# Adding a residual outside the matmul accumulation: x1 rebuilt by rows on GpSimd, added on VectorE

## The chip, the cores and the metric

The kernel runs on one core of a Trainium2 chip. The metric is the device time of one launch in microseconds (us). An execution under the profiler gives the rows that are read below.

## The reference

Sixteen sequences of 256 tokens and 128 channels, float32, go through one block with modulation from a small vector c. For each sequence:

```
h  = layernorm(x) * (1 + ca) + sa
a  = h + linear_attention(h) @ Wo + bo          # 16 heads of 8, elu+1 features
x1 = layernorm(a) * g1 + beta1                  # in the kernel: ny * g1 + beta1
z  = x1 + relu(x1 @ W1 + b1) @ W2 + b2
x  = x + ga * (layernorm(z) * g2 + beta2)
h2 = layernorm(x) * (1 + cb) + sb
x  = x + gb * sigmoid(mix_r(h2) @ Wr) * (square(relu(mix_k(h2) @ Wk)) @ Wv)
```

mix_r and mix_k blend each token with the one before it. The change concerns the x1 in the line of z.

## The kernel before

**Tiles.** A sequence is two chunks (c = 0, 1) of 128 tokens. Tensors "by rows" have tokens on the partitions (ny, z, x2: 128 x 2 x 128); transposed ones have channels on the partitions (hT, x1T: 128 x 256). The normalised rows without gain and shift are called ny. TensorE transposes them into a PSUM bank, and ScalarE turns that into x1T with the gain g1 per partition and the shift beta1 + b2 per partition (L300), so that b2 is already contained in x1T.

**The feed-forward part.** x1T is multiplied with W1 (`hidden_product`, L1018) into four blocks of hid. z is then accumulated in PSUM bank 6. `residual_into` (L980) transposes x1T back into rows as the first write of the accumulation, two 128x128 transposes per sequence; `feed_forward_out` (L986) adds 16 matmul instructions on top (eight products of float32, two instructions each). VectorE reads z out of bank 6 twice: `norm_stats` (L563) for mean and variance, and `centred` (L674), which forms z1 = (z - mean) * row. GpSimd makes rstd_z by a power (`norm_scale`, L453 and L457), and `middle` (L684) forms the new x from z1, rstd_z and xb.

**Stages.** The kernel is a software pipeline over t = 0 to 16, with the order of every engine's instructions written out by hand in a function `step(t)`. In step t, sequence t is at its first norm and attention, t-1 at the second half of attention and at y and ny, t-2 in the feed-forward part up to z, t-3 at z1, x2 and n3, and t-4 at the mixing part and the output. Sequence 15 goes through z in code of its own behind the loop, in chunks.

**Order around the change.** Engines synchronise by semaphores: a signal such as ny_ok is raised once per sequence, and `need(engine, signal, count)` waits for it. VectorE, in step t: stats of z of the previous step (`step_end`), den, rden, z1 (`centred`), att, k, x2 (`middle`), stats of n3, mixT, stats of ny, q, mv of ny, n3, kvs, and last ny (`normalise("ny")`, L578); then the next step starts with the stats of z. GpSimd, in step t: the scale of n1, the gate weights, the scale of n3, the scale of ny (sequence t-1), `plus_row` (L473), xb for t-2 (L484), the scale of z for t-2, and out_sb for t-4 (L491). TensorE starts step t with the transposes of n1, of ny (sequence t-2, written in step t-1) and of n3 (all L975), and ends it with z. In step 8 GpSimd also makes mix_now and mix_prev. ny, z1 and z's bank exist once each; the third of the hidden products of the next sequence goes into bank 6 as well and waits until z has been read (z1_ok).

**Queues.** Most loads are issued by SyncE. ScalarE issues c's columns, bk, bv and the mixing weights at the start.

Of the kernel before, what the change touches and what calls it, by code (L numbers as in the profile page):

```python
# [15 lines left out]
FF = 4  # L16
# [18 lines left out]
def build(nc, a, out, scratch):  # L35
    with ExitStack() as ctx:
# [3 lines left out]
        def sem(name):  # L40
# [62 lines left out]
        hid = sb("hid", [128, FF, L])  # L103
        z1 = sb("z1", [128, NC, D])
        xb = sb("xb", [128, NC, D])
        x2 = [sb(f"x2_{p}", [128, NC, D]) for p in range(2)]
# [51 lines left out]
         prod_ok) = map(sem, ("n1_ok ny_ok n3_ok k_ok q_ok wvm_ok kvs_ok den_ok rden_ok att_ok z1_ok x2_ok mix_ok "  # L158
                              "prod_ok").split())
        stats_ok = {n: sem(f"stats_ok_{n}") for n in NORMS}  # L160
        mv_ok = {n: sem(f"mv_ok_{n}") for n in NORMS}
# [95 lines left out]
        def _(act):  # L257
# [6 lines left out]
            act.wait_ge(pad_ok, 1)  # L264
            act.dma_start(bv_pad[0:1, :], a["bv"].rearrange("(a d) -> a d", a=1)).then_inc(bv_loaded, 16)
            act.dma_start(mix_w[:, :, :], a["mix_w"]).then_inc(mix_loaded, 16)

# [162 lines left out]
        def _(pool):  # L430
# [51 lines left out]
            def x_plus_shift(s, tile):  # L482
# [3 lines left out]
                                        ALU.add).then_inc(xb_ok, 1)  # L486

            def take_out(s):
                need(pool, stored[s % 2], 16 * (s // 2), 16 * S)
                need(pool, prod_ok, s + 1)  # L490
                nc.gpsimd.tensor_tensor(out_sb[s % 2][:, :, :], x2[s % 2][:, :, :], prod[:, :, :], ALU.add).then_inc(out_ok, 1)  # L491

            def step(t):
# [18 lines left out]
                if DIRECT <= t + 1 < S:  # L512
                    plus_row(t + 1)
                if live(t - 2):
                    need(pool, x2_ok, sd)
                    x_plus_shift(sd, xb)
                    if t < S:
                        norm_scale("z", sd + 1)
                    else:
                        tail_scale("z", slice(0, NC), 1)  # L520
# [28 lines left out]
        def _(dve):  # L549
# [25 lines left out]
            def normalise(name, dest, source, count, signal):  # L575
                need(dve, rstd_ok[name], count)
                for c in range(NC):
                    last = nc.vector.tensor_scalar(dest[:, c, :], source(c), mv[name][:, c, 0:1], rstd[name][:, c:c + 1],  # L578
                                                   ALU.subtract, ALU.mult)
                last.then_inc(signal, 1)  # L580
# [83 lines left out]
            def take_n3(t):  # L664
                sp_ = t - 3
                need(dve, h2T_mm, sp_)
                normalise("n3", n3, lambda c: x2[(t - 3) % 2][:, c, :], sp_ + 1, n3_ok)

            def centred(s):
                z = chunked(banks[6])  # L670
                need(dve, mv_ok["z"], s + 1)
                dve.wait_ge(gm_in[part_of(GM_PARTS, s)], 16)
                for c in range(NC):
                    last = nc.vector.scalar_tensor_tensor(z1[:, c, :], z[:, c, :], mv["z"][:, c, 0:1],  # L674
                                                          gm_rows[:, s, G_ROW, :], ALU.subtract, ALU.mult)
                last.then_inc(z1_ok, 1)
# [11 lines left out]
            def step_end(t):  # L688

                sd, sc = t - 2, t - 4  # L690
                z = chunked(banks[6])
                if live(t - 2):
                    need(dve, z_mm, sd + 1)
                    norm_stats("z", lambda c: z[:, c, :])
                if live(t - 4):
                    gated(sc)
                if live(t - 2):
                    norm_mv("z", sd + 1)
# [13 lines left out]
            def step(t):  # L712
                sa, sb_, sd, sp_, sc = t, t - 1, t - 2, t - 3, t - 4
                u = banks[1][:, 0:NC * (D + H)].rearrange("p (c e) -> p c e", c=NC)
                y = chunked(banks[1])
                z = chunked(banks[6])
                x2_p = x2[(t - 3) % 2]
# [156 lines left out]

            z = chunked(banks[6])
            dve.wait_ge(z_mm, LAST)
            norm_stats("z", lambda c: z[:, c, :])
            norm_mv("z", LAST)
# [31 lines left out]
        def _(pe):  # L910
# [72 lines left out]
            def feed_forward_out(f0, f1):  # L983
                for f in range(f0, f1):
                    for c in range(NC):
                        last = nc.tensor.matmul(banks[6][:, c * D:(c + 1) * D], hid[:, f, c * 128:(c + 1) * 128], w2[:, f, :],  # L986
                                                start=False, stop=(f == FF - 1 and c == NC - 1))
                return last
# [24 lines left out]
            def step(t):  # L1013
# [53 lines left out]
                if live(t - 2):  # L1067
# [5 lines left out]
                    if draining(t):  # L1073
                        need(pe, kvs_ok, S)
                        need(pe, hidb_ok, sd)
                    else:
                        need(pe, z1_ok, sd)
                    hidden_product(2)
# [27 lines left out]
                if live(t - 2):  # L1106
                    if draining(t):
                        need(pe, z1_ok, sd)
                        need(pe, hida_ok, sd + 1)
                    else:  # L1110
                        need(pe, hidb_ok, sd + 1)
                    for c in range(NC):
                        residual_into(banks[6], x1T, c)
                if live(t):
# [35 lines left out]
            for f in range(FF):  # L1150
# [3 lines left out]
                if f % 2 == 1:  # L1154
                    last.then_inc((w1a_mm, w1b_mm)[f // 2], 1)
            pe.wait_ge(z1_ok, LAST)
            for c in range(NC):
# [114 lines left out]
```

## Time and profile before

| | us |
|---|---|
| median of 3 runs | 168.03 (167.76 to 170.08) |
| the profiled execution | 168.26 |
| its span in the profile | 166.3 |
| TensorE busy | 157.8 (95%) |
| VectorE busy | 130.5 (78%) |
| ScalarE busy | 119.3 (72%) |
| GpSimd busy | 101.1 (61%) |

The time of an execution is 1.96 us above its span. "Busy" of TensorE counts overlapping matmuls up to the modelled end of each, so the distance between the starts of two groups says what one costs. The granted clock of TensorE is at full speed (1.00, its 2.4 GHz level) in the stretches of the loop. Names in the rows leave out buffer numbers: n1 and n3 both read "n", z1 reads "z", x2 reads "x", wv_gate and the others as they are.

### The profile page before, as it was taken

How to read it: one execution, taken by the hardware profiler on the slowest of the kernel's cores; microseconds unless marked ns; L12 is line 12 of the kernel's file. 1: busy time of each engine (PE TensorE's matmuls, PEld its weight loads, DVE VectorE, ACT ScalarE, POOL GpSimd, SP SyncE). 2: the span in 40 equal slices, each digit the busy share in tenths (PEclk: the TensorE clock that was granted, in tenths of full speed). 3: DMA queues.
4: the chain of work that ended last, by engine and by line, in shares of the span. 5: the costliest groups of instructions: out<-in, count | busy, mean ns of one | idle time of the engine just before them, and what ended most of it. 6: DMA issues, size and time to landing. Idle time of an engine off the chain costs nothing. (4 is left out here: it accounts for less than half of the span.)

```text
span 166.3 us, 4064 instructions
## 1 busy us (share of the span) xinstructions
PE 157.8 (95%) x1155; PEld 145.6 (88%) x1155; DVE 130.5 (78%) x589; ACT 119.3 (72%) x325; POOL 101.1 (61%) x236
## 2 busy tenths in 40 slices
PE   7989799999999999999999999999999999989882
PEld 7867689889999999999999999999999999878571
DVE  3565757789797979798889979897979797977852
ACT  4365685969696969698886969696969694846552
POOL 4333336676576767768597757675767645783531
PEclk9999999999999999999999999999999999999999
DMA  3838929900010101010010101010101010101012
GB/s 114 224 125 267 312 74 307 403 13 0 0 34 4 32 0 34 2 32 3 0 35 0 34 6 32 0 32 4 34 2 35 0 32 0 35 0 35 0 32 63
DMA packets 8173, 9.93 MB, mean 60 GB/s; under 512 B 692, under 2 KB 6360, under 8 KB 8152
## 3 DMA queue, kind: packets, MB, share of 16 engines
q1 hardware_dynamic: 7712, 9.41, 17.9%
q10 hardware_dynamic: 440, 0.28, 0.6%
q8 instruction: 9, 0.15, 0.4%
q14 instruction: 12, 0.10, 0.2%
HBM read 7.55 MB, written 2.13 MB: 58 GB/s over the span
## 5 line engine op out<-in xcount | busy, mean ns | idle before, releaser
L986 PE MATMUL bank<-w,hid 128*128 128x128 f32 x240 | 31.3, 275 | 0.0
L1018 PE MATMUL bank<-x1T,w 128*128 128x256 f32 x120 | 30.9, 380 | 0.0
L986 PEld LDWEIGHTS bank<-w,hid 128*128 128x128 f32 x240 | 29.2, 192 | 0.0
L296 ACT ACTIVATE hT<-bank,modT 128x256 f32<-128x256 f32 x16 | 9.0, 565 | 21.5 <-PE bank L975 21.4
L1018 PEld LDWEIGHTS bank<-x1T,w 128*128 128x128 f32 x120 | 21.5, 190 | 2.5 <-ACT x1T L300 0.2
L457 POOL TENSOR_TENSOR rstd_n<-vare_n,power 128x2 f32<-128x2 f32 x30 | 21.0, 702 | 2.3
L453 POOL TENSOR_TENSOR vare_n<-mv_n,eps 128x2 f32<-128x2 f32 x30 | 6.1, 204 | 20.2 <-DVE mv_n L572 20.2
L274 ACT ACTIVATE n<-x_all,shift_n,rstd_n 128x128 f32<-128x128 f32 x32 | 13.9, 486 | 2.7 <-POOL shift_n L465 2.5
L578 DVE TENSOR_SCALAR ny<-bank,mv_ny,rstd_ny 128x128 f32<-128x128 f32 x32 | 11.7, 406 | 4.6 <-POOL rstd_ny L457 4.2
L288 ACT ACTIVATE keepT<-bank,modT 128x255 f32<-128x255 f32 x28 | 14.3, 562 | 0.6 <-PE bank L975 0.6
L563 DVE BATCH_NORM_STATS2 stats_z<-bank 128x6 f32<-128x128 f32 x30 | 7.4, 289 | 8.5 <-PE bank L986 8.5
L453 POOL TENSOR_TENSOR vare_z<-mv_z,eps 128x2 f32<-128x2 f32 x14 | 2.7, 195 | 18.4 <-DVE mv_z L572 18.4
L975 PE MATMUL bank<-ident,n 128*128 128x128 f32 x62 | 12.1, 276 | 1.4 <-DVE n L578 0.8
L332 ACT ACTIVATE hid<-bank,b_cols 128x256 f32<-128x256 f32 x30 | 12.7, 484 | 0.0
L491 POOL TENSOR_TENSOR out_sb<-x,prod 128x256 f32<-128x256 f32 x15 | 10.9, 728 | 2.1 <-DVE prod L704 2.0
L709 DVE SCALAR_TENSOR_TENSOR mixT<-bank,modT,keepT 128x256 f32<-128x256 f32 x28 | 12.1, 471 | 0.0
L457 POOL TENSOR_TENSOR rstd_ny<-vare_ny,power 128x2 f32<-128x2 f32 x16 | 11.2, 699 | 1.3
L1099 PE MATMUL bank<-kqvo,attT 128*128 128x128 f32 x64 | 11.5, 275 | 0.0
L484 POOL TENSOR_TENSOR xb<-x_all,gm_rows 128x256 f32<-128x256 f32 x15 | 10.9, 724 | 0.2 <-DMA gm_rows<-mod_rows_dram 0.2
L684 DVE SCALAR_TENSOR_TENSOR x<-z,rstd_z,xb 128x128 f32<-128x128 f32 x30 | 10.0, 375 | 0.9 <-POOL out_sb L491 0.7
L300 ACT ACTIVATE x1T<-bank,beta_b,cols 128x256 f32<-128x256 f32 x15 | 8.4, 559 | 3.2 <-PE bank L975 3.2
L563 DVE BATCH_NORM_STATS2 stats_ny<-bank 128x6 f32<-128x128 f32 x32 | 7.8, 287 | 3.6 <-PE bank L1099 2.7
(185 smaller groups left out, 466.7 us busy)
## 6 DMA issues: line engine op xcount, KB each, us to landing
gm_rows<-mod_rows_dram SPq DMA_DIRECT2D x2, 960.0 KB, 8.9
out<-out_sb SPq DMA_DIRECT2D x15, 128.0 KB, 1.8
gm_rows<-mod_rows_dram SPq DMA_DIRECT2D x1, 768.0 KB, 6.1
w<-in_w SPq DMA_DIRECT2D x1, 512.0 KB, 6.7
bv_row<-bv_rows_dram SPq DMA_DIRECT2D x1, 512.0 KB, 10.0
x_all<-in_x SPq DMA_DIRECT2D x1, 384.0 KB, 5.7
bv_row<-bv_rows_dram SPq DMA_DIRECT2D x1, 384.0 KB, 3.5
gm_rows<-mod_rows_dram SPq DMA_DIRECT2D x1, 384.0 KB, 4.3
```

The source lines that it names most:

```text
L274: last = nc.scalar.activation(n1[s % 2][:, c, :], x_all[:, NC * s + c, :], ACT.Identity, scale=rstd["n1"][:, c:c + 1], bias=shift_n1[:, c: ...
L288: nc.scalar.activation(keepT[:, i, 1:L], banks[2][:, 0:L - 1], ACT.Identity, scale=mod_col(KEEP + i, s), bias=mod_col(SB, s)).then_inc((ke ...
L332: last = nc.scalar.activation(hid[:, f, :], hidden_bank(t)[:, (f - 2) * L:(f - 1) * L], ACT.Relu, bias=b1_cols[:, f:f + 1])
L457: nc.gpsimd.tensor_tensor(rstd[name][:, :], vare[name][:, :], power[:, :], ALU.pow).then_inc(rstd_ok[name], 1)
L484: nc.gpsimd.tensor_tensor(tile[:, :, :], x_all[:, NC * s:NC * (s + 1), :], gm_rows[:, s, GB_ROW:GB_ROW + 1, :].broadcast_to([128, NC, D]), ...
L563: ins = nc.vector.bn_stats(stats[name][:, c, :], source(c))
L578: last = nc.vector.tensor_scalar(dest[:, c, :], source(c), mv[name][:, c, 0:1], rstd[name][:, c:c + 1], ALU.subtract, ALU.mult)
L709: nc.vector.scalar_tensor_tensor(mixT[:, i, :], banks[2][:, 0:L], modT[:, MOVE + i, s:s + 1], keepT[:, i, :], ALU.mult, ALU.add).then_inc( ...
L975: last = nc.tensor.transpose(bank[:, c * 128:(c + 1) * 128], tile[:, c, :], ident[:, :])
L986: last = nc.tensor.matmul(banks[6][:, c * D:(c + 1) * D], hid[:, f, c * 128:(c + 1) * 128], w2[:, f, :], start=False, stop=(f == FF - 1 an ...
L1018: return nc.tensor.matmul(bank[:, f % 2 * L:(f % 2 + 1) * L], w1[:, f * 128:(f + 1) * 128], x1T[:, :], start=True, stop=True)
L1099: last = nc.tensor.matmul(banks[1][:, c * D:(c + 1) * D], attT[:, c * 128:(c + 1) * 128], wo, start=False, stop=(c == NC - 1))
```

## The change

x1 is also made by rows. The vectors g1, beta1 and b2 are loaded spread over all partitions. GpSimd multiplies ny by g1 and adds beta1 + b2; VectorE adds the result to z as it copies z from PSUM into a tile z_sb, and both later readers of z take z_sb. TensorE no longer transposes x1T back for sequences 0 to 14; sequence 15 keeps the old way. x1T itself stays, since W1 needs it.

```diff
+        z_sb = sb("z_sb", [128, NC, D])
+        x1_scaled, x1_rows = sb("x1_scaled", [128, NC, D]), sb("x1_rows", [128, NC, D])
+        g1_row, beta1_row, b2_row, shift_row = (sb(n, [128, D]) for n in ("g1_row", "beta1_row", "b2_row", "shift_row"))
...
 # ScalarE's queue, at the start
             act.dma_start(bv_pad[0:1, :], a["bv"].rearrange("(a d) -> a d", a=1)).then_inc(bv_loaded, 16)
+            for row, name in ((g1_row, "g1"), (beta1_row, "beta1"), (b2_row, "b2")):
+                act.dma_start(row[:, :], a[name].rearrange("(a d) -> a d", a=1).broadcast_to([128, D])).then_inc(rows_in, 16)
             act.dma_start(mix_w[:, :, :], a["mix_w"]).then_inc(mix_loaded, 16)
...
 # GpSimd
+            def x1_by_rows(s):
+                if s == 0:
+                    pool.wait_ge(rows_in, 48)
+                    nc.gpsimd.tensor_tensor(shift_row[:, :], beta1_row[:, :], b2_row[:, :], ALU.add).then_inc(shift_row_ok, 1)
+                pool.wait_ge(ny_ok, s + 1)
+                nc.gpsimd.tensor_tensor(x1_scaled[:, :, :], ny[:, :, :], g1_row[:, :].unsqueeze(1).broadcast_to([128, NC, D]),
+                                        ALU.mult).then_inc(x1s_ok, 1)
+                pool.wait_ge(x1s_ok, s + 1)
+                need(pool, zs_ok, s)
+                if s == 0:
+                    pool.wait_ge(shift_row_ok, 1)
+                nc.gpsimd.tensor_tensor(x1_rows[:, :, :], x1_scaled[:, :, :], shift_row[:, :].unsqueeze(1).broadcast_to([128, NC, D]),
+                                        ALU.add).then_inc(x1r_ok, 1)
...
                 if DIRECT <= t + 1 < S:
                     plus_row(t + 1)
                 if live(t - 2):
+                    x1_by_rows(sd)
                     need(pool, x2_ok, sd)
                     x_plus_shift(sd, xb)
...
 # VectorE
             def normalise(name, dest, source, count, signal):
                 need(dve, rstd_ok[name], count)
+                if name == "ny":
+                    need(dve, x1s_ok, count - 1)
...
+            def take_z(s):
+                dve.wait_ge(z_mm, s + 1)
+                dve.wait_ge(x1r_ok, s + 1)
+                nc.vector.tensor_tensor(z_sb[:, :, :], chunked(banks[6]), x1_rows[:, :, :], ALU.add).then_inc(zs_ok, 1)
+                dve.wait_ge(zs_ok, s + 1)
+                norm_stats("z", lambda c: z_sb[:, c, :])
+
             def centred(s):
-                z = chunked(banks[6])
+                z = z_sb
...
 # step_end, VectorE
                 if live(t - 2):
-                    need(dve, z_mm, sd + 1)
-                    norm_stats("z", lambda c: z[:, c, :])
+                    take_z(sd)
...
 # TensorE
-                                                start=False, stop=(f == FF - 1 and c == NC - 1))
+                                                start=(f == 0 and c == 0), stop=(f == FF - 1 and c == NC - 1))
...
                     else:
-                        need(pe, z1_ok, sd)
+                        need(pe, zs_ok, sd)
                     hidden_product(2)
...
-                    for c in range(NC):
-                        residual_into(banks[6], x1T, c)
```

The same replacement of z1_ok by zs_ok is made in the draining step and ahead of sequence 15's own z, and VectorE's code behind the loop calls take_z for sequence 14.

## Rows read from the trace of the kernel before

**Rows 1.** The page, busy time of each engine: us, share of the span, instructions.
```profile
PE 157.8 (95%) x1155; PEld 145.6 (88%) x1155; DVE 130.5 (78%) x589; ACT 119.3 (72%) x325; POOL 101.1 (61%) x236
```

**Rows 2.** Timeline of TensorE: start us, us, engine, line, operation, out<-in, count.
```profile
53.23 0.38 PE L975 MATMUL bank<-ident,ny 128*128 128x128 f32 x2
...
61.99 0.38 PE L975 MATMUL bank<-ident,ny 128*128 128x128 f32 x2
```

**Rows 3.** Timeline of TensorE: the residual's transposes and the group behind them.
```profile
59.08 0.38 PE L980 MATMUL bank<-ident,x1T 128*128 128x128 f32 x2
59.30 0.41 PE L1120 MATMUL bank<-wv_plus,a_sb 128*128 128x144 f32 x2
```

**Rows 4.** Timeline of VectorE, one period.
```profile
53.21 0.49 DVE L563 BATCH_NORM_STATS2 stats_z<-bank 128x6 f32<-128x128 f32 x2 [0.79 <-PE bank L986]
...
55.08 0.51 DVE L674 SCALAR_TENSOR_TENSOR z<-bank,mv_z,gm_rows 128x128 f32<-128x128 f32 x2
...
55.91 0.42 DVE L767 SCALAR_TENSOR_TENSOR k_sb<-exp_k,bank 128x256 f32<-128x256 f32 x1
56.24 0.61 DVE L684 SCALAR_TENSOR_TENSOR x<-z,rstd_z,xb 128x128 f32<-128x128 f32 x2
...
58.07 0.24 DVE L572 BATCH_NORM_AGGREGATE mv_n<-stats_n 128x2 f32<-128x6 f32 x2
58.40 0.49 DVE L563 BATCH_NORM_STATS2 stats_ny<-bank 128x6 f32<-128x128 f32 x2
...
59.14 0.24 DVE L572 BATCH_NORM_AGGREGATE mv_ny<-stats_ny 128x2 f32<-128x6 f32 x2
...
60.46 0.73 DVE L578 TENSOR_SCALAR ny<-bank,mv_ny,rstd_ny 128x128 f32<-128x128 f32 x2 [0.19 <-POOL rstd_ny L457]
61.98 0.49 DVE L563 BATCH_NORM_STATS2 stats_z<-bank 128x6 f32<-128x128 f32 x2 [0.79 <-PE bank L986]
```

**Rows 5.** Timeline of GpSimd in the same period and the next.
```profile
55.20 0.73 POOL L491 TENSOR_TENSOR out_sb<-x,prod 128x256 f32<-128x256 f32 x1
...
59.46 0.20 POOL L453 TENSOR_TENSOR vare_ny<-mv_ny,eps 128x2 f32<-128x2 f32 x1
59.73 0.69 POOL L457 TENSOR_TENSOR rstd_ny<-vare_ny,power 128x2 f32<-128x2 f32 x1
...
60.80 0.73 POOL L484 TENSOR_TENSOR xb<-x_all,gm_rows 128x256 f32<-128x256 f32 x1
63.03 0.19 POOL L453 TENSOR_TENSOR vare_z<-mv_z,eps 128x2 f32<-128x2 f32 x1 [1.50 <-DVE mv_z L572]
```

**Rows 6.** Timeline of VectorE, then of GpSimd, in the step with mix_prev.
```profile
82.55 1.20 DVE L684 SCALAR_TENSOR_TENSOR x<-z,rstd_z,xb 128x128 f32<-128x128 f32 x2
...
82.89 0.72 POOL L528 TENSOR_TENSOR mix_prev<-mix_w,mix_now 128x256 f32<-128x256 f32 x1
```

**Rows 7.** Timeline of ScalarE at the start.
```profile
5.85 0.88 ACT L274 ACTIVATE n<-x_all,shift_n,rstd_n 128x128 f32<-128x128 f32 x2 [2.51 <-POOL shift_n L465]
```

**Rows 8.** Timeline of VectorE, steps 2 to 4 and the last period's end.
```profile
25.66 0.25 DVE L572 BATCH_NORM_AGGREGATE mv_ny<-stats_ny 128x2 f32<-128x6 f32 x2
...
27.63 0.48 DVE L563 BATCH_NORM_STATS2 stats_z<-bank 128x6 f32<-128x128 f32 x2
...
32.78 0.49 DVE L563 BATCH_NORM_STATS2 stats_ny<-bank 128x6 f32<-128x128 f32 x2 [0.77 <-PE bank L1099]
...
35.49 0.48 DVE L563 BATCH_NORM_STATS2 stats_z<-bank 128x6 f32<-128x128 f32 x2
...
44.44 0.50 DVE L563 BATCH_NORM_STATS2 stats_z<-bank 128x6 f32<-128x128 f32 x2 [0.76 <-PE bank L986]
...
141.29 0.50 DVE L563 BATCH_NORM_STATS2 stats_z<-bank 128x6 f32<-128x128 f32 x2 [0.79 <-PE bank L986]
```

**Rows 9.** Timeline of VectorE, then of GpSimd, in the last step.
```profile
147.76 0.73 DVE L578 TENSOR_SCALAR ny<-bank,mv_ny,rstd_ny 128x128 f32<-128x128 f32 x2 [0.89 <-POOL rstd_ny L457]
...
148.61 0.72 POOL L484 TENSOR_TENSOR xb<-x_all,gm_rows 128x256 f32<-128x256 f32 x1
```

More of the change, by code:

```diff
@@ L159, in build @@
                               "prod_ok").split())
+        rows_in, shift_row_ok, x1s_ok, x1r_ok, zs_ok = map(sem, "rows_in shift_row_ok x1s_ok x1r_ok zs_ok".split())
         stats_ok = {n: sem(f"stats_ok_{n}") for n in NORMS}
@@ L690, in step_end @@
                 sd, sc = t - 2, t - 4
-                z = chunked(banks[6])
                 if live(t - 2):
-                    need(dve, z_mm, sd + 1)
-                    norm_stats("z", lambda c: z[:, c, :])
+                    take_z(sd)
                 if live(t - 4):
@@ L715, in step @@
                 y = chunked(banks[1])
-                z = chunked(banks[6])
                 x2_p = x2[(t - 3) % 2]
@@ L873, in out_of_last @@
                                         ALU.add).then_inc(out_last_ok[c], 1)
-            z = chunked(banks[6])
-            dve.wait_ge(z_mm, LAST)
-            norm_stats("z", lambda c: z[:, c, :])
+            take_z(LAST - 1)
             norm_mv("z", LAST)
@@ L1107, in step @@
                     if draining(t):
-                        need(pe, z1_ok, sd)
+                        need(pe, zs_ok, sd)
                         need(pe, hida_ok, sd + 1)
@@ L1155, in _ @@
                     last.then_inc((w1a_mm, w1b_mm)[f // 2], 1)
-            pe.wait_ge(z1_ok, LAST)
+            pe.wait_ge(zs_ok, LAST)
             for c in range(NC):
@@ L1259 @@
         "bv": attn["bv"],
+        "g1": attn["g1"],
+        "beta1": attn["beta1"],
+        "b2": attn["b2"],
     }
```

## The prediction

> **What bounds the kernel now.** I first read the busy totals: TensorE 95%, VectorE 78%, GpSimd 61% [rows 1]. That suggests that work taken off TensorE is gained and that GpSimd has room for more; whether it is so depends on where the work is put, so I went to the timeline of one step, engine by engine. On TensorE the transposes of ny start at 53.23 and 61.99: a period of 8.76 to 8.77 us with no idle time noted between them [rows 2]. VectorE shows the same 8.77 us from stats_z to stats_z (53.21 to 61.98), and in it a wait of 0.79 us for TensorE's z [rows 4]. From 44.44 to 141.29 [rows 8] there are eleven such periods, ten of 8.77 and one of 9.15 (the step in which GpSimd also makes mix_now and mix_prev). So TensorE sets the pace, but its lead is small: ny ends at 61.19 (60.46 + 0.73) and TensorE reads it at 61.99, a margin of 0.80 us [rows 2, 4].
>
> **TensorE's saving.** A pair of residual transposes moves the next group's start from 59.08 to 59.30 [rows 3]: 0.22 us per step, 15 steps, 3.3 us in all, if TensorE stays the bound. One matmul's duration there is no price, since they overlap (the pair lasts 0.38 us). The Trainium skill (TensorE: Matmul & The Clock Gate, Part 4: PE-mode transpose) gives about 275 ns for one transpose in a kernel; two of them per step would make the saving 8.3 us by that figure, and the start-to-start row decides against it.
>
> **The new wait of ny.** This is the step that decides. There is one buffer ny, and normalise("ny") of sequence t-1 now waits until GpSimd has read the ny of t-2 (x1s_ok). GpSimd does that reading in the same step t, behind the scale of ny (t-1) and plus_row. So ny (t-1) can't be written when its rstd is ready, but only after plus_row and a whole 128x256 pass.
> I count from the end of mv_ny, 59.14 + 0.24 = 59.38. Before: vare_ny at +0.08, ny at +1.08 [rows 4, 5]. New: x1_scaled starts where xb starts now, 60.80, +1.42; xb is the same form with a broadcast row, 0.73 us [rows 5], so it ends at +2.15; ny starts at +2.19 (a wait across engines costs 0.04, as rstd_ny to ny). That is 1.11 later, against a margin of 0.80, and ny ends at +2.92.
> x1_rows is one more 0.73: it waits for x1_scaled on its own engine (about 0.08, the spacing between vare and its rstd) and runs from +2.23 to +2.95. xb, and then vare_z, are queued behind both; vare_z was preceded by 1.50 us of idle time [rows 5], 1.46 of which x1_rows and x1_scaled take, and it waits for a later mv_z now anyway: nothing.
>
> **VectorE's add.** take_z needs x1_rows: it starts at +2.99. Nearest row: k_sb, 128x256 with one operand in PSUM, 0.42 us [rows 4]. Then a wait on its own result, 0.04: stats_z starts at +3.45. Before it was 61.98 - 59.38 = +2.60, of which 0.79 was the wait for TensorE. The cover of the add is thus gone.
> From stats_z to the end of mv_ny VectorE is in order and nearly gapless: 59.38 - 53.21 = 6.17, less 0.17 of waiting for y (stats_ny starts 0.33 after mv_n, where 0.16 is the usual spacing), 6.00 [rows 4]. The new loop is 6.00 + 3.45 = 9.45 us, against 8.55 for TensorE. bn_stats I take as equal from either memory, but z1 read from z_sb should look like x (0.61 a pair with SBUF operands) and not like z1 now (0.51) [rows 4]: +0.10, so 9.55.
>
> **z1 against GpSimd's out_sb.** z1 now takes z and the row both from SBUF. Where x, with the same operands, met mix_prev on GpSimd, its pair took 1.20 us instead of 0.61 and ended at 83.75, 0.14 after mix_prev [rows 6, 4]. In the ordinary step x meets only 128x2 instructions of GpSimd, and its 0.61 is undisturbed. z1 starts at 1.87 after stats_z and out_sb at 1.99 (55.08 and 55.20) [rows 4, 5], both hung on the same stats_z, so they will meet in every step. The first half of z1 is under way, the second waits until out_sb's 0.73 is over and ends at about +2.86 instead of +2.38: 0.48 in place of the 0.10, a period of 9.93. Bounds: 0 (GpSimd yields) to 0.75 (both halves wait). I take 0.48, the measured pattern.
> The Trainium skill (SBUF — State Buffer, Who interferes with whom) says that a VectorE instruction with two SBUF inputs and a GpSimd instruction that reads SBUF exclude each other; the trace agrees for x (1.20 against 0.61), and no row shows it for z1.
>
> **Start.** Three more loads are issued on ScalarE's queue, 64 KB written each. ScalarE's n1 waits 2.51 us for GpSimd there [rows 7]; three issues of up to 0.8 us each would fit. Their traffic beside x and the weights: 0 to 0.7 us, taken as 0. They are needed at 27 us, long landed. The first shift_row (128x128, 0.42) lies once in front of x1_scaled. In step 2 mv_ny ends at 25.91 and stats_z starts at 27.63, +1.72; new +3.45 + 0.42: 2.15 later. Step 3 is bound by latency (VectorE waits 0.77 for y) and gets the 1.1 of ny again; step 4, 35.49 to 44.44 = 8.95, becomes 9.5 [rows 8]. Together 3.7 us (rounded).
>
> **Middle.** Eleven periods at 9.93 = 109.2; less 0.42 in the last, which has no plus_row; plus 0.6 in the step with mix_prev, whose x is delayed as before but with no slack to take it: 109.4 against 96.85, +12.5.
>
> **End.** In the last step GpSimd scales n3 between ny and x1_scaled: x1_scaled takes xb's place at 148.61, ends at 149.34, and ny starts at 149.38 instead of 147.76 [rows 9]: +1.6. ny, n3, x and the last norms follow one another on VectorE from there, so the add counts too: +0.5. Total +2.1.
>
> **Sum.** 3.7 + 12.5 + 2.1 = 18.3 on the profiled execution's 168.26: 186.6. The median of the runs is 168.03, 0.23 lower: 186.3 us, 11% slower. TensorE's 3.3 us and the earlier release of z's bank (after the add instead of after z1) are worth nothing, as TensorE then waits 9.93 - 8.55 = 1.4 us per step for ny.
>
> **Rivals.**
> 1. The loop, without the meeting of z1 and out_sb (period 9.55): 11 x 0.38 = 4.2 less, 182.1. For it: which of the two waits depends on 0.12 us. Chance 0.27.
> 2. VectorE's order gives way and only the path through TensorE counts: ny's transposes to y's stats 5.17 (53.23 to 58.40), from there to the mean 0.98, then +2.95: 9.10 per period. 3.6 in the middle, 2.6 at the start, 2.1 at the end: about 176.5. Against it: VectorE's 6.00 has no gaps that I can see. Chance 0.09.
> 3. Not slower: GpSimd gets to x1_scaled early, so that the wait on x1s_ok is over before rstd_ny. TensorE stays the bound and saves up to 3.3 us: 164.7 to 168. It decides whether x1_scaled ends before 60.42 in a step like this one; GpSimd does have idle time (1.50 us), but after xb and not before, and its order is written out. Chance 0.08, half of it for a saving of 2% or a little more.
> 4. Worse than 190: GpSimd's two passes also hold up n3 or q on VectorE, or the first loads are late. Chance 0.06.
> My forecast has 0.50. The change does what it says: no rival there beyond the residual being free on TensorE, which is in rival 3.
>
> **Range and chances.** 2% is about what a measurement of this kernel can tell from no change: 164.7 to 171.4. Faster 0.04, within 0.05, slower 0.91. The range of 181 to 190 takes in the forecast with its upper bound for z1 (0.27 x 11 = 3 us more) and rival 1, and leaves out rivals 2 to 4.
>
> **What the changed profile would show.** TensorE's period about 9.9 us, with an idle time before the transposes of ny whose releaser is VectorE's ny; VectorE idle 1.2 us before ny, released by x1_scaled on GpSimd; no wait of VectorE for z's matmuls in the middle; z1 near 0.9 to 1.0 us a pair (0.6 in rival 1); the add at 0.42. I am wrong if x1_scaled stands ahead of rstd_ny, or if the periods stay below 9 us.

## The result: 14% slower, more than predicted

The changed kernel takes 191.95 us (median of four runs, 190.64 to 193.28) against 167.89 for the kernel before: a ratio of 1.1385 (95% interval 1.1315 to 1.1454). The forecast was 186.3 with a range of 181 to 190. The sign and the waits that make the loss came out as predicted; the size did not, and the time lies above the range. Medians here and below are over all executions, ratios leave out the few that fell in a slower state.

The profiled execution took 190.64 us with a span of 188.9, against 168.26 and 166.3 before. I split the 22.6 us between the spans at the same two events as the forecast, the start of stats_z in the fourth and in the fifteenth step [rows 8]: 4.0 at the start (48.41 against 44.44), 15.75 in the middle (48.41 to 161.01 is 112.6, against 96.85), 2.9 at the end. Predicted: 3.7, 12.5 and 2.1. The missing 4.3 us of the sum is therefore mostly in the middle.

Busy time of each engine, from the page after:

```profile
PE 161.6 (86%) x1125; PEld 142.7 (76%) x1125; DVE 140.6 (74%) x604; ACT 121.6 (64%) x325; POOL 125.6 (66%) x267
```

VectorE gained 10.1 us of work and GpSimd 24.5 [rows 1]; yet VectorE's share of the span fell from 78% to 74% and GpSimd's rose only from 61% to 66%, since the span grew too. No engine is near 100%. The loop is now a chain that passes from engine to engine, and the waits show it. (In the rows x1_scaled reads "x_scaled" and x1_rows "x_rows"; wv_plus is what plus_row writes.) From the list of waits (waiter, waited for, us in total, times, longest):

```profile
POOL vare_n L459 <- DVE mv_n L593: 23.8, 16, 4.3
DVE ny L601 <- POOL x_scaled L499: 21.2, 15, 2.6
```

VectorE's timeline, one period:

```profile
79.20 0.49 DVE L584 BATCH_NORM_STATS2 stats_z<-z_sb 128x6 f32<-128x128 f32 x2
...
81.06 0.99 DVE L704 SCALAR_TENSOR_TENSOR z<-z_sb,mv_z,gm_rows 128x128 f32<-128x128 f32 x2
...
84.67 0.46 DVE L584 BATCH_NORM_STATS2 stats_ny<-bank 128x6 f32<-128x128 f32 x2
85.05 0.41 DVE L749 SCALAR_TENSOR_TENSOR qT<-exp_q,relu_q 128x256 f32<-128x256 f32 x1
85.38 0.24 DVE L593 BATCH_NORM_AGGREGATE mv_ny<-stats_ny 128x2 f32<-128x6 f32 x2
...
88.22 0.73 DVE L601 TENSOR_SCALAR ny<-bank,mv_ny,rstd_ny 128x128 f32<-128x128 f32 x2 [1.29 <-POOL x_scaled L499]
89.02 0.42 DVE L695 TENSOR_TENSOR z_sb<-bank,x_rows 128x256 f32<-128x256 f32 x1
89.47 0.49 DVE L584 BATCH_NORM_STATS2 stats_z<-z_sb 128x6 f32<-128x128 f32 x2
```

GpSimd's timeline in the same period:

```profile
81.18 0.72 POOL L511 TENSOR_TENSOR out_sb<-x,prod 128x256 f32<-128x256 f32 x1
...
85.11 0.90 POOL L463 TENSOR_TENSOR rstd_n<-vare_n,power 128x2 f32<-128x2 f32 x1
85.97 0.19 POOL L459 TENSOR_TENSOR vare_ny<-mv_ny,eps 128x2 f32<-128x2 f32 x1
86.24 0.76 POOL L463 TENSOR_TENSOR rstd_ny<-vare_ny,power 128x2 f32<-128x2 f32 x1
86.97 0.45 POOL L479 TENSOR_TENSOR wv_plus<-wv_mod,bv_row 128x128 f32<-128x128 f32 x1
87.39 0.72 POOL L499 TENSOR_TENSOR x_scaled<-ny,g_row 128x256 f32<-128x256 f32 x1
88.19 0.72 POOL L505 TENSOR_TENSOR x_rows<-x_scaled,shift_row 128x256 f32<-128x256 f32 x1
```

And TensorE:

```profile
89.00 0.44 PE L1000 MATMUL bank<-ident,ny 128*128 128x128 f32 x2 [0.83 <-DVE ny L601]
```

The period is 10.27 us, from 79.20 to 89.47, in place of 8.77. The chain reads: mean of ny (ends 85.62), vare_ny (85.97), rstd_ny, plus_row, x1_scaled (87.39 to 88.11), then x1_rows on GpSimd beside ny on VectorE, the add (89.02), stats_z (89.47). TensorE, which had no idle time noted before the transposes of ny [rows 2], sits still there for 0.83 us.

### The profile page after: what moved, and what is told of

Its sections match the earlier page's. It is cut to its first block and busy times, and to the rows that moved or that the text cites. A ratio compares the mean times of both kernels' runs of the same rounds, so it can differ in the third digit from the quotient of the medians.

```text
span 188.9 us, 4098 instructions
## 1 busy us (share of the span) xinstructions
PE 161.6 (86%) x1125; PEld 142.7 (76%) x1125; DVE 140.6 (74%) x604; ACT 121.6 (64%) x325; POOL 125.6 (66%) x267
## 5 line engine op out<-in xcount | busy, mean ns | idle before, releaser
L463 POOL TENSOR_TENSOR rstd_n<-vare_n,power 128x2 f32<-128x2 f32 x30 | 23.4, 779 | 2.4
L1000 PE MATMUL bank<-ident,ny 128*128 128x128 f32 x32 | 7.0, 301 | 16.5 <-DVE ny L601 16.5
L1000 PEld LDWEIGHTS bank<-ident,ny 128*128 128x128 f32 x32 | 3.2, 140 | 20.1 <-DVE ny L601 20.1
L704 DVE SCALAR_TENSOR_TENSOR z<-z_sb,mv_z,gm_rows 128x128 f32<-128x128 f32 x30 | 13.4, 488 | 0.0
L601 DVE TENSOR_SCALAR n<-x,mv_n,rstd_n 128x128 f32<-128x128 f32 x28 | 8.5, 347 | 6.3 <-POOL rstd_n L463 6.3
L463 POOL TENSOR_TENSOR rstd_ny<-vare_ny,power 128x2 f32<-128x2 f32 x16 | 11.9, 742 | 1.3
L505 POOL TENSOR_TENSOR x_rows<-x_scaled,shift_row 128x256 f32<-128x256 f32 x15 | 10.8, 722 | 1.2
L332 ACT ACTIVATE attT<-bank 128x256 f32<-128x256 f32 x16 | 6.1, 383 | 8.5 <-PE bank L1000 8.4
```

Source lines behind the costliest of these rows:

```text
L463: nc.gpsimd.tensor_tensor(rstd[name][:, :], vare[name][:, :], power[:, :], ALU.pow).then_inc(rstd_ok[name], 1)
L505: nc.gpsimd.tensor_tensor(x1_rows[:, :, :], x1_scaled[:, :, :], shift_row[:, :].unsqueeze(1).broadcast_to([128, NC, D]), ALU.add).then_inc ...
L1000: last = nc.tensor.transpose(bank[:, c * 128:(c + 1) * 128], tile[:, c, :], ident[:, :])
```

## The experiments

Each ran beside the kernel before on the same chip. A ratio is to that kernel, with its 95% interval. Periods are stats_z to stats_z in an ordinary step of the middle.

**Do the two passes cost anything by themselves?** The kernel before, with two passes of the same shape on GpSimd where x1_by_rows stands. They read x_all, and nobody waits for them.

```diff
                 if live(t - 2):
+                    <x_all rows * row -> x1_scaled, + row -> x1_rows>
                     need(pool, x2_ok, sd)
```

> The kernel before, with two more 128x256 passes on GpSimd where x1_by_rows stands; they read x_all and a row of gm_rows and write tiles that nobody reads, so nobody waits for them. Theory: the passes as such are free, since the 1.50 us of idle time before vare_z takes their 1.46 us: 168 to 169 us, period 8.77, TensorE bound. Rival: GpSimd's load or its port is what costs (out_sb and the scale of n1 pushed late, VectorE's SBUF reads blocked): over 171 us, with a period over 8.95.

Measured: 169.03 us, ratio 1.006 (1.0043 to 1.0076), profiled 168.90; the period stayed at 8.76 to 8.77. VectorE, then GpSimd:

```profile
62.05 0.50 DVE L571 BATCH_NORM_STATS2 stats_z<-bank 128x6 f32<-128x128 f32 x2 [0.79 <-PE bank L994]
...
70.81 0.50 DVE L571 BATCH_NORM_STATS2 stats_z<-bank 128x6 f32<-128x128 f32 x2 [0.79 <-PE bank L994]
```
```profile
62.35 0.73 POOL L486 TENSOR_TENSOR xb<-x_all,gm_rows 128x256 f32<-128x256 f32 x1
63.10 0.19 POOL L455 TENSOR_TENSOR vare_z<-mv_z,eps 128x2 f32<-128x2 f32 x1
```

vare_z follows xb without a gap, and stands 1.05 us behind the start of stats_z as before: the passes filled the idle time in front of it [rows 5]. In an ordinary step 1.5 us more work on GpSimd costs nothing as long as nobody waits for it; in the whole kernel it cost 1 us.

**Then the waits alone.** The same two passes, plus VectorE's wait for x1_scaled before ny and for x1_rows before stats_z; the residual stays on TensorE, and there is no add.

```diff
+                if name == "ny":
+                    need(dve, x1s_ok, count - 1)
...
                     need(dve, z_mm, sd + 1)
+                    dve.wait_ge(x1r_ok, sd + 1)
```

> The kernel before, with TensorE's residual in place and z read from PSUM as there, plus the two passes on GpSimd (on x_all, for nobody's use) and the two waits of VectorE on them: ny on the first, the stats of z on the second. No add, no z_sb. Theory: the waits alone make the loop: the changed kernel's 10.28 less the add and its wait (0.46) and less what z1 loses to out_sb (0.48): period 9.35, and with TensorE's 8.77 below it the time is 168.3 + 11 x 0.58 + 3 at the start + 1.6 at the end = 179 to 180. Rival: the waits only matter together with the add, since VectorE has 0.79 us of idle time in front of the stats of z: period 8.8 to 9.1 and under 176.

Measured: 182.33 us (181.11 to 183.47), ratio 1.0799 (1.0675 to 1.0924); the kernel before was at 169.74 there. Periods of 9.25 us, with 9.3 to 9.45 in three of them. VectorE's timeline:

```profile
63.40 0.24 DVE L580 BATCH_NORM_AGGREGATE mv_ny<-stats_ny 128x2 f32<-128x6 f32 x2
...
65.89 0.73 DVE L588 TENSOR_SCALAR ny<-bank,mv_ny,rstd_ny 128x128 f32<-128x128 f32 x2 [1.41 <-POOL x_scaled L520]
66.69 0.49 DVE L571 BATCH_NORM_STATS2 stats_z<-bank 128x6 f32<-128x128 f32 x2
```

So more than half of the loss needs no new work on VectorE at all, only the place of the two passes in GpSimd's order: 13.1 us between the spans (179.4 against 166.3). The shares differ by stage. The start (stats_z of the fourth step at 48.14) and the end (28.4 us from that of the fifteenth) cost about as much as in the change, 3.7 and 3.4 us; the middle costs 6.0 of the 15.75.

**The add alone.** The changed kernel without the passes and their waits. take_z adds the rows of x_all instead of x1's; this kernel leaves x1 out of z.

```diff
-                    x1_by_rows(sd)
...
-                dve.wait_ge(x1r_ok, s + 1)
-                nc.vector.tensor_tensor(z_sb[:, :, :], chunked(banks[6]), x1_rows[:, :, :], ALU.add)
+                nc.vector.tensor_tensor(z_sb[:, :, :], chunked(banks[6]), x_all[:, NC * s:NC * (s + 1), :], ALU.add)
```

> The changed kernel without GpSimd's two passes and without both waits on them; VectorE adds x_all's rows in place of x1's, so the output leaves out x1 and takes x there. TensorE's residual stays away. Theory: the add with its cover gone and z1 against out_sb still cost more than TensorE gives: stats_z to the mean of ny 6.0 + 0.48, from there 2.7 to the next stats_z: period 9.15 us, 172 to 174. Rival: VectorE has room for the add and only GpSimd's passes are the cause: TensorE sets the period at 8.55, 165 to 166.

Measured: 174.44 us, ratio 1.035 (1.0281 to 1.0419), period 9.25. VectorE, and TensorE in the same period:

```profile
70.85 0.24 DVE L592 BATCH_NORM_AGGREGATE mv_ny<-stats_ny 128x2 f32<-128x6 f32 x2
...
73.46 0.42 DVE L691 TENSOR_TENSOR z_sb<-bank,x_all 128x256 f32<-128x256 f32 x1 [0.22 <-PE bank L1007]
...
75.88 0.99 DVE L700 SCALAR_TENSOR_TENSOR z<-z_sb,mv_z,gm_rows 128x128 f32<-128x128 f32 x2
```
```profile
67.98 0.44 PE L996 MATMUL bank<-ident,att 128*128 128x128 f32 x2 [0.38 <-DVE att L751]
```

Waits alone +0.48 per period, add with z1 from z_sb +0.48, both together +1.50 (10.27 against 8.77). Each alone is partly covered by the 0.79 us for which VectorE used to wait for TensorE [rows 4]: with the waits alone nothing is left of it, with the add alone 0.22. Together they can't both hide in it. The two kernels are also bound by different loops. With the waits alone it is the loop of VectorE and GpSimd. With the add alone the loop goes through TensorE: the add and the longer z1 stand before att, TensorE waits 0.38 us for att, and VectorE then waits for TensorE's z. This kernel showed something else too. GpSimd:

```profile
70.58 0.90 POOL L463 TENSOR_TENSOR rstd_n<-vare_n,power 128x2 f32<-128x2 f32 x1
...
71.45 0.19 POOL L459 TENSOR_TENSOR vare_ny<-mv_ny,eps 128x2 f32<-128x2 f32 x1
```

The mean of ny ends at 71.09, and vare_ny starts 0.36 later, behind a long rstd_n, without any pass of x1 on GpSimd. In the kernel with the waits alone, where stats_ny still waits for y, it starts 0.08 after the mean (63.72 against 63.64). So this delay belongs to the part with the add and not to the passes; it matters below.

**Is it the single buffer ny?** Two buffers, and the wait before ny loosened by one sequence.

```diff
-        ny = sb("ny", [128, NC, D])
+        ny = [sb(f"ny{p}", [128, NC, D]) for p in range(2)]
-                    need(dve, x1s_ok, count - 1)
+                    need(dve, x1s_ok, count - 2)
```

> The changed kernel with two ny buffers, so that VectorE's ny waits for the x1_scaled of one sequence earlier, which is long done. Theory: the loop has two equal branches behind x1_scaled, ny and x1_rows with take_z; taking the first away leaves take_z at the end of x1_rows, 0.07 us sooner than now. Period 10.2 us instead of 10.28; VectorE idle before the add instead of before ny, TensorE idle moved behind it. About 1 us less in the loop, 2 us less in the last step, where ny of sequence 15 no longer waits: 187 to 188.5 beside the 190.64 of the changed kernel's profiled execution. Rival: the wait on ny alone is the cause; then the period falls to about 9.0 us and the time to 175 to 178.

Measured: 191.47 us, ratio 1.1402 (1.1339 to 1.1464), as slow as the change; period 10.27. VectorE:

```profile
87.61 0.73 DVE L601 TENSOR_SCALAR ny<-bank,mv_ny,rstd_ny 128x128 f32<-128x128 f32 x2
...
89.58 0.42 DVE L695 TENSOR_TENSOR z_sb<-bank,x_rows 128x256 f32<-128x256 f32 x1 [1.24 <-POOL x_rows L505]
```

ny no longer waits, and 1.24 us of idle time stand before the add instead. The two waits are two branches that end within 0.1 us of each other, both behind x1_scaled; taking one away shows the other. The 2 us that I expected from the last step did not show either.

**Is it the meeting of z1 and out_sb?** GpSimd takes out_sb before the scale of z, when z1 has not begun.

```diff
+                if live(t - 4) and t < S:
+                    take_out(sc)
                 if live(t - 2):
                     <scale of z>
-                if live(t - 4):
+                if live(t - 4) and t == S:
                     take_out(sc)
```

> The changed kernel with out_sb ahead of the scale of z on GpSimd, so that it runs under mv_z and the stats of n1 and not under z1. Theory: z1's pair falls from 0.99 to 0.61 us, the period from 10.28 to 9.9, the time by 11 x 0.38 = 4.2 us to 186 to 187. Rival: z1 is slow by reading both operands from SBUF, whatever GpSimd does: z1 stays near 0.99 and the time at 190.6. Second rival: rstd_z comes too late for x2 (out_sb now stands before it), and x2 waits what z1 saves: also no gain, but z1 at 0.61.

Measured: 186.78 us, ratio 1.1136 (1.1104 to 1.1168), period 9.80. GpSimd's out_sb and VectorE's z1:

```profile
78.74 0.73 POOL L511 TENSOR_TENSOR out_sb<-x,prod 128x256 f32<-128x256 f32 x1 [0.83 <-DVE prod L735]
```
```profile
79.66 0.51 DVE L707 SCALAR_TENSOR_TENSOR z<-z_sb,mv_z,gm_rows 128x128 f32<-128x128 f32 x2
```

z1 is back at 0.51 and the period 0.47 shorter: the meeting costs what the forecast said. Away from out_sb, z1 from two SBUF operands takes 0.51, no more than from PSUM.

**Is it q, under way when GpSimd starts n3's scale?** In the change, rstd_n takes 0.90 where it took 0.69 in the period of before. The edit puts q_elu ahead of y_stats.

```diff
+                if live(t) and not (t < 3):
+                    q_elu()
                 if live(t - 1) and not y_first:
                     y_stats()
-                if live(t) and not (t < 3):
-                    q_elu()
```

> The changed kernel with q (two SBUF operands, 0.41 us) ahead of the stats of ny on VectorE. Theory: GpSimd's rstd_n lasts 0.90 instead of 0.69 us because q holds the port when it starts (q 85.05, rstd_n 85.11); moved away, rstd_n falls to 0.70, vare_ny and all behind it come 0.2 us sooner, period 10.08, time 188 to 189 beside 190.64. Rival: the 0.90 comes from somewhere else: no change, rstd_n still 0.90.

Measured: 189.56 us, ratio 1.1296 (1.1255 to 1.1337), period 10.16. GpSimd:

```profile
85.05 0.69 POOL L463 TENSOR_TENSOR rstd_n<-vare_n,power 128x2 f32<-128x2 f32 x1
85.76 0.19 POOL L459 TENSOR_TENSOR vare_ny<-mv_ny,eps 128x2 f32<-128x2 f32 x1
```

rstd_n is back at 0.69, but vare_n before it now runs beside q and takes 0.28, and the gain is 0.11 a period. The mean of ny ends at 85.68 here, so vare_ny is at +0.08 again, and from the mean to stats_z it is 3.53 us instead of 3.85. So the second part gained 0.32 and the first, from stats_z to the mean, lost 0.21 (6.63 instead of 6.42): q ahead of y_stats makes the mean itself later.

**The passes a step earlier.** x1 of sequence t-1 is made right behind xb of t-2, when ny of t-1 has just been written.

```diff
                 if live(t - 2):
-                    x1_by_rows(sd)
                     need(pool, x2_ok, sd)
                     x_plus_shift(sd, xb)
+                if live(t - 1) and t < S:
+                    x1_by_rows(sb_)
```

> The changed kernel with x1_by_rows moved on GpSimd: both passes for sequence t-1 now stand in step t behind xb and ahead of the scale of z, so they are done a step before VectorE needs them; everything else as changed. Theory: the 1.6 us of x1_scaled and x1_rows leave the path from the mean of ny to the stats of z. That path falls from 3.85 to 2.7 us (vare_ny at 0.35, ny at 1.42 and 0.73 long, the add 0.42), z1 no longer meets out_sb, the period becomes 8.8 us, and the time 168 to 171. Rival: GpSimd's load bounds the loop wherever the passes stand (its instructions sum to about 8.3 us, and vare_z now waits for them): period 9.3 or more, over 174 us.

Measured: 172.9 us, ratio 1.0266 (1.0189 to 1.0342). The waits of ny and of the add for GpSimd's passes are gone. Six of the eleven periods are 9.25 to 9.32 us, four are 8.81 or 8.82, and the one with mix_prev is 9.77. TensorE and VectorE in a long one:

```profile
76.30 0.44 PE L1002 MATMUL bank<-ident,att 128*128 128x128 f32 x2 [0.38 <-DVE att L757]
```
```profile
74.82 1.02 DVE L706 SCALAR_TENSOR_TENSOR z<-z_sb,mv_z,gm_rows 128x128 f32<-128x128 f32 x2
```

I had expected 8.8 throughout. In the long periods z1 still meets out_sb (0.99 to 1.07 for the pair), and att, next on VectorE, reaches TensorE late; in the short ones z1 takes 0.51.

**With q ahead of y_stats as well.**

> The kernel with the early x1 rows, and q ahead of the stats of ny on VectorE as well. Theory: without q in its way rstd_n lasts 0.69, the mean of ny isn't kept waiting for it, and the path to the next stats_z is 2.35: period 8.6, close to TensorE's 8.55, time 165.5 to 167.5, the first version at or below the 168 of the kernel before. Rival: z1 and x, with two SBUF operands each, meet other passes of GpSimd in the new order; then the period stays at 8.8 to 9.1 and the time at 168 to 172.

Measured: 175.93 us, ratio 1.0405 (1.0335 to 1.0474), a steady period of 9.25: slower than without it, and a clear miss: I had expected 8.6 and 165.5 to 167.5. z1 takes 0.99 to 1.03 here in every period of the middle.

**With out_sb ahead as well** (passes early, out_sb first, q early), and the same with q left in its place:

> The kernel with the early x1 rows and the early q, and out_sb ahead of the scale of z as well. In e7 TensorE waits 0.38 us for att in every step, since z1, ahead of att on VectorE, takes 0.99 us beside out_sb, and the period is 9.25. Theory: with out_sb away from z1 that wait goes, the path from the mean of ny to the stats of z is 2.35 and the rest 6.1 to 6.2: period 8.55 to 8.7, TensorE bound, 165.5 to 167.5, at or below the kernel before. Rival: out_sb now pushes rstd_z behind x on VectorE, or the two passes meet another read; then the period stays above 8.9 and the time above 170.

> As the kernel with early rows, early q and early out_sb, but with q in its old place, under rstd_n. Theory: rstd_n 0.90 instead of 0.69 keeps the mean of ny waiting as in the changed kernel; path 2.7, period 8.8, 168 to 170. Rival: TensorE is the bound by then and hides it: same time as with the early q.

Measured: 171.42 us, ratio 1.0189 (1.0144 to 1.0234), and 171.86, ratio 1.0206 (1.0164 to 1.0248). Their periods are 8.77 and 8.80, where I had expected 8.55 to 8.7 of the first. VectorE and TensorE of the first:

```profile
66.33 0.48 DVE L759 TENSOR_TENSOR att<-bank,rden 128x128 f32<-128x128 f32 x2
...
72.34 0.42 DVE L699 TENSOR_TENSOR z_sb<-bank,x_rows 128x256 f32<-128x256 f32 x1 [0.19 <-PE bank L1015]
...
74.67 0.52 DVE L708 SCALAR_TENSOR_TENSOR z<-z_sb,mv_z,gm_rows 128x128 f32<-128x128 f32 x2
```
```profile
66.86 0.44 PE L1004 MATMUL bank<-ident,att 128*128 128x128 f32 x2
```

Nearly all of the loss in the middle is gone with two moves of GpSimd's work (97.65 us against 96.85; 97.23 with the early q as well), and VectorE waits for TensorE's z again. Of the 3.4 us by which the first one's span is longer than before, 2.0 are there at 46.48, the stats_z that stood at 44.44 before [rows 8], 0.4 more come in the steps around mix_prev, 1.0 behind the stats_z of the fifteenth step. It doesn't win, though TensorE has 0.22 us less to do per step: small gaps in TensorE's issue give it back. Set against the starts of TensorE's groups before, they are 0.12 us around the transposes of att and 0.11 around the products of mixT, both just written by VectorE. Before, att ended at 55.99 and TensorE took it at 56.44; here it ends at 66.81 and is taken at 66.86. The add and its hand-over, 0.46 us ahead of att on VectorE, have used up that margin, and the loop stats_z, att, TensorE's z, add closes at 8.77. That is read from the rows; no run tests it.

**How much is there to win at all?** The kernel before without the residual's transposes, and with nothing in their place; z leaves out x1 in sequences 0 to 14.

```diff
-                    for c in range(NC):
-                        residual_into(banks[6], x1T, c)
```

> The kernel before without TensorE's residual transposes and with nothing in their place, so z leaves out x1 in sequences 0 to 14: the most that the change could gain. Theory: TensorE sets the period, which falls from 8.77 to 8.55 (0.22 less), 15 times: 3.3 us less, 164.5 to 165. Rival: a chain through VectorE and GpSimd is just behind (ny's margin was 0.80 us) and takes part of it: 165.5 or more.

Measured: 166.19 us, ratio 0.9898 (0.9842 to 0.9954), period 8.55. VectorE:

```profile
61.19 0.49 DVE L563 BATCH_NORM_STATS2 stats_z<-bank 128x6 f32<-128x128 f32 x2 [0.57 <-PE bank L986]
...
69.74 0.49 DVE L563 BATCH_NORM_STATS2 stats_z<-bank 128x6 f32<-128x128 f32 x2 [0.57 <-PE bank L986]
```

8.77 less 0.22, the start-to-start price of the pair [rows 3]. The whole fell by 1.8 us in the median (2.6 between this span and that of before), less than the 3.3 us that I had expected. Even for free, the change is worth 1%. By the 275 ns per transpose of the Trainium skill (TensorE: Matmul & The Clock Gate, Part 4: PE-mode transpose) an estimate would have been 8.3 us; the runs decide against that figure as a price in a stream.

**The end.** In the last step TensorE is idle for 2.6 us before the transposes of ny, and behind it its granted clock falls. Matmuls whose result nobody reads were put in front of that wait.

```diff
-            pe.wait_ge(ny_ok, S)
             pe.wait_ge(hida_ok, LAST)
+            keep_warm(11)
+            pe.wait_ge(ny_ok, S)
             transpose_in(banks[7], ny, x1T_mm)
```

> The changed kernel with 11 idle matmuls on TensorE (2.4 us) ahead of the last step's wait for ny, where it stood idle from 167.9 to 170.5 and the granted clock fell to 0.57 of full speed in the 4 us behind. Theory: the clock stays at full speed there, the eight matmuls of the last hidden block take 1.9 instead of 3.0 us, and the profiled execution is 0.5 to 1 us shorter (190 us, span 188), with runs closer together. Rival: the clock isn't tied to that idle time; no change beyond 0.2 us and the same 3.0 us.

Measured: 192.58 us, ratio 1.1413 (1.1343 to 1.1483): no gain in the whole. TensorE of the change, and then of this kernel:

```profile
170.54 0.44 PE L1000 MATMUL bank<-ident,ny 128*128 128x128 f32 x2 [2.62 <-DVE ny L601]
...
171.80 3.04 PE L1175 MATMUL bank<-x1T,w 128*128 128x256 f32 x8
```
```profile
174.27 1.89 PE L1176 MATMUL bank<-x1T,w 128*128 128x256 f32 x8
```

The added matmuls did keep the clock (1.00 of full between 172 and 180 us), and the eight matmuls took 1.89, as before the change. But from the stats_z of sequence 14 (171.84 in the change, 174.30 here) to the end it was 16.7 us against 17.1, so 0.4 us came of it. This execution had begun 2.3 us later by the first stats_z, which hides it in the total.

**The start: the three loads.** They were moved behind ScalarE's first step.

> The changed kernel with the three row loads issued by ScalarE at the end of step 0 instead of before mix_w. Theory: the loads cost nothing in either place; the first step's VectorE den starts near 14 us in the one and the other, and the time is the changed kernel's, 190.6 to 193.3. Rival: their traffic beside the first weights and x delays the start by up to 2 us in some executions; then the late loads give 190.6 in all runs, with the start always near 14 us.

Measured: 191.28 us, ratio 1.1364 (1.1313 to 1.1415), no different from the change. The first den came at 15.81 us in its profiled execution, and at 13.98 in that of the change, which issues the loads early (14.27 before). The kernel with the added matmuls issues them early as well and had it at 16.25. So executions differ by about 2 us at the start, and the loads' place is not why. What is, stays open.

## Why the prediction was right, and where it failed

**TensorE's saving: right.** 0.22 us per step, as the run without the residual shows, and not collected. I had all of TensorE's waiting, 1.4 us, before ny; it is 0.83 there and 0.35 for att, which I had not seen.

**The waits behind x1_scaled: right.** Predicted idle time of VectorE before ny 1.2 us, measured 1.29. That plus_row and a pass stand before ny, and x1_rows before the add, is the mechanism of the loss; it goes when the passes move (periods of 8.8 to 9.3), and not when the wait of ny alone is loosened. xb and vare_z at nothing: right; vare_z still waits 0.92 us for mv_z.

**The add: right,** 0.42. **z1: right in the sum.** 0.99 for the pair in place of 0.51. I had it as 0.10 for SBUF operands and 0.38 more for out_sb; the first is nothing, the meeting is all of it.

**The step that failed: "before: vare_ny at +0.08", carried over unchanged to the new loop.** In the period of before, stats_ny waits for TensorE's y, 0.17 us. I took that wait out of the sum (6.17 to 6.00) for VectorE and did not ask what GpSimd is doing when the mean comes earlier. It is still at n3's scale. That scale is also longer: in the change q (85.05) starts just before rstd_n (85.11) and rstd_n takes 0.90. In the ordinary period of before, rstd_n starts first and takes 0.69. So GpSimd comes to vare_ny 0.35 after the mean, 0.27 later than forecast: 0.21 of it is the longer rstd_n, the rest the earlier mean. The trace of before held the answer in one of its periods. In the second period behind the one with mix_prev, stats_ny did not wait for y either. VectorE, then GpSimd:

```profile
102.68 0.46 DVE L563 BATCH_NORM_STATS2 stats_ny<-bank 128x6 f32<-128x128 f32 x2
103.06 0.41 DVE L722 SCALAR_TENSOR_TENSOR qT<-exp_q,relu_q 128x256 f32<-128x256 f32 x1
103.39 0.24 DVE L572 BATCH_NORM_AGGREGATE mv_ny<-stats_ny 128x2 f32<-128x6 f32 x2
```
```profile
103.12 0.90 POOL L457 TENSOR_TENSOR rstd_n<-vare_n,power 128x2 f32<-128x2 f32 x1
103.98 0.19 POOL L453 TENSOR_TENSOR vare_ny<-mv_ny,eps 128x2 f32<-128x2 f32 x1
```

q stands before rstd_n, rstd_n takes 0.90, and vare_ny comes 0.35 after the mean, as later in the change; there VectorE's spare time hid it. rstd_ny takes 0.76 instead of 0.69 as well, in the change and in that period, where it starts 0.13 us behind n3's pair instead of 0.28; what holds it up is not shown. My rival 4, at 0.06, came nearest, but it had the passes as the cause and VectorE's q as the one held up. It is GpSimd that is held up, and it needs only that stats_ny no longer waits, as the add-alone kernel shows, which has it without the passes.

The second, smaller miss is the hand-over: from the end of a 128x256 pass to the instruction that waits for it, 0.11 us (x1_scaled ends at 88.11, ny starts at 88.22), where I took the 0.04 of rstd_ny to ny. In all, 3.85 us from the mean to stats_z instead of 3.45 (0.27, 0.07 of rstd_ny and 0.07 of the hand-over); and 6.42 instead of 6.48 before it. A period of 10.27 for 9.93 [rows 4, 5].

**The sum of the middle.** Eleven periods of 0.34 more are 3.7; the step with mix_prev took 0.46 more than an ordinary one instead of 0.6, and the last 0.84 less instead of 0.42. That leaves 3.2, which is 112.6 against 109.4.

**Start: right** (4.0 for 3.7, though its three terms, 2.15, 1.1 and 0.55, add up to 3.8), the loads included: den of the first step is no later than before. The upper bound of 0.7 us for their traffic had no row behind it.

**End:** 0.8 more than forecast. ny waits 2.57 us for x1_scaled, and from the mean to ny it is 1.7 us more than before, for 1.6 forecast. But the mean itself comes 0.6 later behind the last period's stats_z (161.01 to 166.99, against 141.29 to 146.67), and I had no term for that. z1 meets GpSimd's gate weights and xb_last there, and its pair takes 1.36 us instead of 0.60:

```profile
163.66 1.36 DVE L704 SCALAR_TENSOR_TENSOR z<-z_sb,mv_z,gm_rows 128x128 f32<-128x128 f32 x2
```

In all kernels here that read z from PSUM this pair takes 0.60, also beside the two passes, and in all that read z_sb at least 1.26. It is the kind of meeting that I had priced for the loop and left out of the last step. From ny on it is 0.6 more than before, for 0.5 forecast. The windows of 4 us in the last step (us, busy time and count of PE, PEld, DVE, ACT and POOL, granted clock, DMA share, GB/s) show what is in that part:

```profile
168.00:172.00 4.00, 0.91 (x5) 0.67 (x6) 2.21 (x7) 0.56 (x1) 2.98 (x6) 1.00 0.00 0
172.00:176.00 4.00, 4.00 (x16) 3.29 (x15) 3.01 (x14) 2.52 (x6) 1.43 (x2) 0.57 0.12 33
```

TensorE did little in the first window, and was granted 0.57 of full speed in the second, most of it at the lower of its two levels, 1.2 GHz. Holding it at 2.4 GHz gave 0.4 us back, so the clock is the larger share of these 0.6. I had given 0.5 to the add alone.

**The median.** The profiled execution was the fastest of four, 1.3 us below their median. I had put the median 0.23 below the profile's time, as with the kernel before. This is the rest of the miss: 4.0 in the sum (4.3 between the spans, less 0.2, since the execution took 1.74 us more than its span and not 1.96), 1.3 and 0.23 here, 5.6 in all.

**The range** gave 3 us upwards for the meeting of z1 alone, and nothing for GpSimd's order or for the spread of the runs. 190 was too near to the forecast: each of eleven equal periods multiplies an error of 0.1 us to more than 1 us.

## What to carry to other kernels

When an edit removes or shortens a wait, look at the other engine's queue at the new, earlier time: a gap that a row shows between a result and its reader (+0.08 here) holds only for the old arrival. Work on an engine with idle time is nearly free until somebody waits for it; two passes of the same shape cost 1 us in the whole kernel when nobody did, and moving them behind the next thing in the queue, out of the chain, took away most of a loss of 14%. A cover is spent once: two edits that cost 0.48 each alone cost 1.50 together. And look for the odd period in the trace of before: one of eleven had the order of the new loop and showed its price.

## What the runs showed of the hardware

VectorE operations with two operands in SBUF and GpSimd operations held each other up in both directions, and small ones too. VectorE lost when GpSimd's pass began during the pair: z1 0.51 to 0.99 beside out_sb, as x had [rows 6]. GpSimd lost when VectorE was first: its 128x2 rstd_n took 0.90 instead of 0.69 beside q, in eleven steps of the change in a row and once in the kernel before (103.12), and its vare_n 0.28 instead of 0.20 with q ahead of y_stats. The Trainium skill (SBUF — State Buffer, Who interferes with whom) says that issue order decides who blocks, and the runs agree as to rstd_n: where q began after it, before the change, it kept its 0.69. But q lost nothing there either. VectorE and GpSimd, before:

```profile
58.81 0.41 DVE L722 SCALAR_TENSOR_TENSOR qT<-exp_q,relu_q 128x256 f32<-128x256 f32 x1
```
```profile
58.66 0.69 POOL L457 TENSOR_TENSOR rstd_n<-vare_n,power 128x2 f32<-128x2 f32 x1
```

q begins 0.15 us into a rstd_n that runs until 59.35, ends at 59.22, and takes 0.41 us, as in the change, where it is first. So a small GpSimd operation did not keep VectorE out for its whole length; beside the 128x256 out_sb the pair of z1 ended only at 82.05, 0.15 behind out_sb's end at 81.90.

Not expected: reading z from SBUF is no slower than from PSUM when undisturbed (0.51 both for z1, 0.49 both for stats_z), so the difference between x (0.61) and z1 (0.51) is not the place of the operands.
